# Summing the GpSimd-multiplied states of a selective scan: an accumulating DMA issued from GpSimd before the identity matmuls

## What is computed

```python
x = silu(conv1d(xz[..., :1024]));  z = xz[..., 1024:]
Bm, Cm = split(x @ W_x, 2)                  # 16 columns each
delta = softplus(x @ W_dt + b_dt)
def step(h, t):
    dA = exp(delta_t[:, :, None] * A[None])
    dBu = delta_t[:, :, None] * B_t[:, None, :] * u_t[:, :, None]
    h = dA * h + dBu
    y = einsum('bds,bs->bd', h, C_t)        # sum over the 16 states
    return h, y
y = (y + x * D) * silu(z)
out = y @ W_out + residual
```

## Time and profile before

| | us |
|---|---|
| median of 2 runs | 5908.1 (5903.17 to 5913.04) |
| profiled execution, its time | 5908.51 |
| its span from first to last instruction | 5906.7 |
| busy: PE / DVE / POOL / ACT | 5489.1 / 5072.9 / 4435.4 / 3314.7 |

### The profile page before, as it was taken

The page is one execution under the profiler, slowest core; times in us unless marked ns, Lnnn a source line. Parts: engine busy times, 40 slices in busy tenths (PEclk is TensorE's granted clock), DMA queues, the critical chain, the costliest instruction groups (busy, mean ns, idle before and its releaser), DMA issues. The chain is left out here.

```text
span 5906.7 us, 84901 instructions
## 1 busy us (share of the span) xinstructions
PE 5489.1 (93%) x23552; PEld 4380.9 (74%) x23552; DVE 5072.9 (86%) x9455; ACT 3314.7 (56%) x7923; POOL 4435.4 (75%) x2807
## 2 busy tenths in 40 slices
PE   7999789999999999999999999999999999979999
PEld 6777567777777777777777777777777777757777
DVE  6888589999999989999999899989989899966775
ACT  4444256666666656665666565666666565644443
POOL 2223179999999999999999999999999999951110
PEclk9999899999999999999999999999999999989999
DMA  3221311111111111111111111111111111121111
GB/s 91 74 85 71 119 44 40 49 58 46 41 40 40 40 41 40 41 40 41 40 41 40 41 40 45 50 43 58 47 41 40 41 40 41 40 93 43 57 57 43
DMA packets 140217, 299.07 MB, mean 51 GB/s; under 512 B 23425, under 2 KB 41889, under 8 KB 139681
## 3 DMA queue, kind: packets, MB, share of 16 engines
q1 hardware_dynamic: 139680, 293.09, 14.8%
HBM read 223.79 MB, written 69.27 MB: 50 GB/s over the span
## 5 line engine op out<-in xcount | busy, mean ns | idle before, releaser
L868 POOL TENSOR_TENSOR mx_dbu<-mx_bs,mx_du 128x1024 f32<-128x1024 f32 x1024 | 2417.9, 2361 | 306.7 <-DVE mx_hp L1069 278.2
L971 ACT ACTIVATE mx_ps_da<-mx_dl,mx_a 128x256 f32<-128x256 f32 x4096 | 1748.4, 464 | 1375.6 <-DVE mx_hc L1084 1322.5
L1069 DVE TENSOR_TENSOR_SCAN mx_ps_da<-mx_ps_da,mx_hst,mx_dbu 128x256 f32<-128x256 f32 x2048 | 1424.0, 740 | 111.1 <-ACT mx_hst L932 37.5
L1069 DVE TENSOR_TENSOR_SCAN mx_hp<-mx_ps_da,mx_hst,mx_dbu 128x256 f32<-128x256 f32 x2048 | 1399.4, 724 | 19.1 <-ACT mx_ps_da L971 19.1
L847 POOL TENSOR_TENSOR mx_hp<-mx_hp,mx_cs 128x512 f32<-128x512 f32 x1024 | 1306.2, 1276 | 0.4 <-ACT mx_hst L932 0.4
L1264 PE MATMUL mx_ps_y<-mx_hp,mx_ident 128*128 128x256 f32 x4096 | 1062.9, 382 | 1.8 <-issue 1.6
L1255 PE MATMUL mx_ps_y<-mx_hc,mx_ident 128*128 128x256 f32 x4096 | 1055.4, 380 | 7.8 <-DVE mx_gy L1055 6.0
L1232 PE MATMUL mx_ps_m<-mx_u,mx_w_dt 128*128 128x256 f32 x4144 | 997.2, 384 | 41.2 <-issue 25.8
L1232 PEld LDWEIGHTS mx_ps_m<-mx_u,mx_w_dt 128*128 128x128 f32 x4144 | 794.5, 192 | 199.2 <-issue 90.4
L1264 PEld LDWEIGHTS mx_ps_y<-mx_hp,mx_ident 128*128 128x128 f32 x4096 | 785.7, 192 | 119.2 <-issue 5.7
L1255 PEld LDWEIGHTS mx_ps_y<-mx_hc,mx_ident 128*128 128x128 f32 x4096 | 780.9, 191 | 119.4 <-DVE mx_hc L1084 9.3
(11 more groups left out here) (95 smaller groups left out, 7157.2 us busy)
## 6 DMA issues: line engine op xcount, KB each, us to landing
mx_bs<-bc_scratch SPq DMA_DIRECT2D x132, 512.0 KB, 3.7
mx_cs<-bc_scratch SPq DMA_DIRECT2D x132, 512.0 KB, 4.8
mx_hT<-hT_scratch SPq DMA_DIRECT2D x34, 518.0 KB, 6.0
f_x<-in_L_attn_inp SPq DMA_DIRECT2D x16, 1024.0 KB, 5.3
xs_scratch<-f_x SPq DMA_DIRECT2D x16, 1024.0 KB, 4.3
hT_scratch<-f_h2T SPq DMA_DIRECT2D x16, 1024.0 KB, 5.4
mx_xo<-xs_scratch SPq DMA_DIRECT2D x32, 512.0 KB, 5.9
x_scratch<-mx_xo SPq DMA_DIRECT2D x32, 512.0 KB, 2.8
```

What stands on the lines that cost most here:

```text
L868: G.tensor_tensor(dbu[:, n % NM], bs[:, g], bcast(du[:, b % 2, :], SG), ALU.mult).then_inc(s_m1, 1)
L971: ins = A.activation(ps_da[DA_BANK[p]][:, k, :], dl[:, b % NL, :], ACT.Exp, scale=a_sb[:, b, s:s + 1])
L1069: ins = V.tensor_tensor_scan(da if half == 0 else hp[:, n % NH, k, :], da, dbu[:, n % NM, s, :], hst[:, b, SG * g + s:SG * g + s + 1], ALU ...
```

## The change

`sum_states` goes. Two neighbouring units q and q+1 (q even) lie side by side in the ring, and after both are multiplied by C, GpSimd issues one DMA that adds state k = 1 of both to state k = 0 of both, in place. TensorE waits for that DMA and sums only k = 0. Each of the four pairs of ring places has its own semaphore. GpSimd's `dbu` of each odd unit now waits for GpSimd's own multiply of unit n-4. The sum from `hp` comes one unit later (SUM_LAG 6), for two units at once.

```diff
+        s_f = [sem(f"states_folded{n}") for n in range(NH // 2)]
...
-        KEEP_LAG, PAIR_LAG, SUMC_LAG, SUM_LAG = 2, 3, 2, 5
+        KEEP_LAG, PAIR_LAG, FOLD_LAG, SUMC_LAG, SUM_LAG = 2, 3, 5, 2, 6
...
+            def fold(c, q):
+
+                at = q % NH
+                pool.dma_start(hp[:, at:at + 2, 0, :], hp[:, at:at + 2, 1, :], accum_op=ALU.add).then_inc(s_f[at // 2], 16)
...
                     if not (is0(i) and n < NM):
                         pool.wait_ge(s_sc, 2 * NU * i + 2 * (n - NM + 1))
+                    if not (is0(i) and n < FOLD_LAG) and (n - FOLD_LAG) % 2 == 0:
+                        pool.wait_ge(s_pr, NU * i + (n - FOLD_LAG + 2))
                     G.tensor_tensor(dbu[:, n % NM], bs[:, g], bcast(du[:, b % 2, :], SG), ALU.mult).then_inc(s_m1, 1)
+                    if n >= FOLD_LAG and (n - FOLD_LAG) % 2 == 0:
+                        fold(i, n - FOLD_LAG)
+                    elif not is0(i) and (n - FOLD_LAG) % 2 == 0:
+                        fold(i - 1, NU + n - FOLD_LAG)
...
-            def sum_states(c, n):
-
-                b, g = divmod(n, NG)
-                pe.wait_ge(s_pr, NU * c + (n + 1))
-                for k in range(SG - SD):
-                    ins = M.matmul(ps_y[b % 2][:, 0:T], ident[:, :], hp[:, n % NH, k, :],
-                                   start=False, stop=(g == NG - 1 and k == SG - SD - 1), skip_group_check=True)
-                ins.then_inc(s_r, 1)
+            def sum_folded(c, q):
+
+                b, g = divmod(q, NG)
+                at = q % NH
+                pe.wait_ge(s_f[at // 2], 16 * NU // NH * c + 16 * (q // NH + 1))
+                for n in range(2):
+                    ins = M.matmul(ps_y[b % 2][:, 0:T], ident[:, :], hp[:, at + n, 0, :],
+                                   start=False, stop=(g + n == NG - 1), skip_group_check=True)
+                ins.then_inc(s_r, 2)
...
-                    if n >= SUM_LAG:
-                        sum_states(i, n - SUM_LAG)
-                    elif not is0(i):
-                        sum_states(i - 1, NU + n - SUM_LAG)
+                    if n >= SUM_LAG and (n - SUM_LAG) % 2 == 0:
+                        sum_folded(i, n - SUM_LAG)
+                    elif not is0(i) and (n - SUM_LAG) % 2 == 0:
+                        sum_folded(i - 1, NU + n - SUM_LAG)
```

More of the change, by code:

```diff
@@ L879, in epilogue @@
                 for n in range(NU):
+                    if n < FOLD_LAG and (n - FOLD_LAG) % 2 == 0:
+                        pool.wait_ge(s_pr, NU * (LAST + 1) + (n - FOLD_LAG + 2))
+                        fold(LAST, NU + n - FOLD_LAG)
                     if n < PAIR_LAG:
@@ L1317, in epilogue @@
                         out_product(LAST, LAST % 2, j, range(ND))
-                    if n < SUM_LAG:
-                        sum_states(LAST, NU + n - SUM_LAG)
+                    if n < SUM_LAG and (n - SUM_LAG) % 2 == 0:
+                        sum_folded(LAST, NU + n - SUM_LAG)
                     if n < SUMC_LAG:
```

## The result

The changed kernel takes 6358.7 us (6356.35 to 6361.11, 2 runs) against 5908.1: ratio 1.0756, 95% interval 1.0734 to 1.0777. It is 7.6% slower; 6388 was forecast, in a range of 6020 to 7150.

The account below looks back on a forecast made before the run. GpSimd's queue was to set the pace, TensorE being late only once a chunk. A chunk of 134.7 + 16 D us, 155.2 at D = 1.28 against 140.2, adds 479 us: 6388 us, range 6020 to 7150.

Parts of the forecast that it names:

- D: GpSimd's time to issue one fold's DMA, taken as 1.28 us, with ends 0.39 and 2.36; 16 folds a chunk.
- The own wait: GpSimd's wait for its own multiply ahead of each odd unit's `dbu`: 0.2 us each, 3.2 us a chunk.
- GpSimd's wait for VectorE: Idle time ahead of `dbu` behind VectorE's scans, 260.5 us in 4000; to vanish but for 0.4 us a chunk.
- The later order of the sums: TensorE's sum from `hp` coming one unit later (SUM_LAG 6), costed at nothing.
- The late gate product would come early enough: TensorE saves 13.8 us a chunk, more than VectorE's 7.7 us gate wait; at most 246 us in all.
- the first rival: GpSimd issues the DMA cheaply and time does not rise: 5932 at D = 0.39, 5732 at 0; chance 0.10.
- the break-even at D = 0.34: Issue time of one fold on GpSimd at which the change neither gains nor loses, from 512 D - 176 us.
- Cheap issue: GpSimd hands the DMA over as SP does, in 0.39 us, time 5932; chance 0.10, 0.03 of it faster.
- Landing: The DMA's landing paces TensorE and VectorE if over 14.8 us; at 20 the time is 7695; chance 0.06.
- Clock: TensorE's granted clock falls as it idles; at half the time low, chunk 170 us, time 6860; chance 0.05.
- The gate wait gone: Sign of being right: VectorE's wait of 7.4 us at the gate disappears.
- A gap near 1.3 us at the fold: Sign of being right: median gap on GpSimd between the `dbu` before and the multiply behind a fold.

Follow-up runs that it names:

- e4: Kernel before with all its sums, plus the same adding DMA on a spare buffer, without the wait for GpSimd's multiply: 6293.8 us, 1.0663.
- e7: Changed kernel with GpSimd's wait for its own multiply and the DMA moved one instruction later: 6317.7 us, ratio 1.0689.
- e5: Kernel before with only the sums' order changed: four states of a pair summed together, a unit later, no DMA: 5932.4 us, 1.0035.
- e1: Changed kernel without the DMA and GpSimd's wait for its own multiply; TensorE sums k = 0 alone: 5838.8 us, ratio 0.9883.
- e2: Changed kernel without the DMA, GpSimd's wait for its own multiply kept; TensorE sums k = 0 alone: 5848.1 us, ratio 0.9899.
- e10: Kernel before plus 16 plain copies a chunk on the spare buffer, issued from SP: 5906.4 us, ratio 1.0003.
- e9: e4 with a plain copy in place of the adding DMA, still issued from GpSimd: 6103.9 us, ratio 1.0329.
- e3: Changed kernel with the DMA adding on a spare buffer and TensorE waiting for GpSimd's multiply, not the DMA: 6375.5 us, ratio 1.0788.
- e6: Changed kernel with the ring laid out state by state, so each DMA adds 128 rows of 2 KB, not 256 of 1 KB: 6198.6 us, 1.0488.
- e8: Changed kernel with both the state-by-state ring and the own wait and DMA moved one instruction later: 6135.0 us, ratio 1.0379.

## Why the prediction was right

**The sum.** The mechanism held: GpSimd's queue sets the pace, and each fold costs it the time of the DMA's record. Of the size, GpSimd's rows give the account, in us a chunk. Forecast were 150.2 of work (129.7 + 16 x 1.28) and 5.0 of idle time; measured are 4270.0/28.7 = 149.0 and 130.0/28.7 = 4.5. D was chosen by the nearest row, a multiply of 512 columns; the record's median is 1.197, and e4 gives 1.18 by the length of the chunks, so D was 0.08 too much. The own wait was put at 3.2. Of GpSimd's 130 us of idle time the two named parts leave 44, 1.5 a chunk, and e7 prices the wait at 1.3. The price of one wait was right and their number was not: in 315 of the 459 folds of this stretch `dbu` follows the multiply directly and starts 1.42 us after it (median), where 1.23 is usual; in 114 the addition of the logarithm stands between, and the wait costs nothing. Against this, GpSimd's wait for VectorE was to vanish but for 0.4, and 49.1/28.7 = 1.7 stayed; the wait for `du` grew from 0.9 to 1.3, and that for the logarithm, 0.5, went. Over 32 chunks this is 38 us less work and 16 less idle time than forecast, so +425 in place of +479.

From the first `dbu` to the last the program took 434 us more than before (781.0 to 5683.9, against 775.8 to 5244.5). Another 18 us, 5 ahead of that and 13 behind it, lie where the forecast had nothing, and no row here says why. So 452 us by the spans, for 479. Errors of both signs met, the largest -54 us (the own wait), -38 (D) and +42 (the wait for VectorE); that the size came within 30 us is in part luck. The later order of the sums, taken as nothing, costs 21 us in e5, where TensorE is late; in the changed kernel the wait that it caused is absent (0.4 us).

**Which wait is late.** "The late gate product would come early enough" was wrong. It was worked out by comparing a chunk's saving (13.8 us) with a chunk's stall (7.7 us); e1 shows 2.2 us come back, since the stall is shortened only by what leaves TensorE's unbroken work ahead of it, 2.6 us of the 13.8. In the changed kernel the gate wait is still 140.1/28.7 = 4.9 us a chunk. The forecast did not rest on it, but the first rival did: at D = 0 it gave 5732 and 3% faster, and e2, which is the changed kernel at D = 0, shows 5848. So the formula, which lets GpSimd's wait for VectorE vanish, holds only where the folds are dear enough, and the break-even at D = 0.34 is not supported.

**The rivals.** Cheap issue: SP's issue of the same 256 rows is free here (e10), GpSimd's is not, even for a plain copy (e9, 0.75 us). The lower end of D, 0.39, was itself too low: SP takes 0.594 us for these rows. The rule of the Trainium skill ("DMA: Bandwidth & Descriptors", section "Issuing engines are not separate DMA queues") that the time to initiate a DMA is usually small beside the DMA itself does not hold for this case: 1.20 us of GpSimd against 3.8 us to landing, and the 3.8 are hidden while the 1.20 are not. The estimate from the first-byte figures of the Trainium skill ("DMA: Bandwidth & Descriptors", section "Latency and other measured facts"), D = 0.79 and 6137, came out between the copy's 0.75 and the addition's 1.20 and missed the addition. Landing: it takes 3.8 us at the median and 9.6 at most, under the 14.8 us allowed, and e3 excludes it. Clock: the granted clock did fall, from 0.99 to 0.93 in the mixer. TensorE is busy 83% there and is waited for no more than before (ScalarE's wait for the gate product is 8.5 us a chunk, 8.6 before), so it is not the bound; no run held the clock fixed, so a small share of it stays open.

**What was to be seen.** GpSimd's wait for VectorE nearly gone: from 9.1 us a chunk to 1.7, right in the main. The gate wait gone: wrong, 4.9 us a chunk are left. VectorE waiting some 20 us a chunk for `dbu`: the right wait, but 12.8 us. 2048 records over `hp`: right. A gap near 1.3 us at the fold: wrong as a gap, since the multiply started 0.77 us behind the DMA's start and the rest travelled along as lag. A D of another size was to move the time by 512 us for each microsecond: e6 moved it by 160 for 0.315, which is 508.

## What to carry to other kernels

Before moving work off the busiest engine, find the stall that it causes, follow the engine back from there to its own last wait, and count only what leaves the work between the two; a total over the chunk says little. A DMA issued from GpSimd is an instruction of GpSimd and is priced as one; here it cost more with more rows, and for the same rows an addition cost more than a copy. So give it few long rows, and try few of them first: two folds a chunk gained 0.9%, where sixteen in the same layout (e8) lost 3.8%. If a plain copy will do, issue it from an engine that has time, as SP had here.

## What the runs showed of the hardware that was not expected

- An adding DMA on GpSimd costs 1197 ns at 256 rows of 1 KB and 882 at 128 of 2 KB; the line through both, an estimate, is 0.57 us and 2.5 ns a row. A plain copy of 256 rows costs 747 ns and goes out in 80 packets in place of 272.
- An adding DMA holds up the next instruction's start for 0.77 us only, and lengthens those behind it by 0.43 us until one waits for GpSimd's own result. Two DMAs without such a wait between them leave twice that: in e4 a multiply behind the second took 2.13 us, where 1.27 is its length.
- The wait for the predecessor's result leaves 0.16 us idle where GpSimd has work queued (`du` ahead of `dbu`); 512 such waits in a kernel where it has time to spare (e2) cost 9 us, which the spread of the runs covers.
- 512 copies of 256 KB in SBUF from SP, issued in 0.594 us each, left the time as it was (ratio 0.9994 to 1.0012).
